# Scores of an attention block: two heads side by side in fp32r instead of one head in bf16 parts

## The reference

```python
q, k, v = (split_heads(einsum('bsd,kd->bsk', x, w)) for w in (wq, wk, wv))   # 16 heads of 8
scores = einsum('bhtc,bhkc->bhtk', q, k) * 8 ** -0.5
attn = softmax(where(causal, scores, -inf))
x = layernorm(x + einsum('bsv,dv->bsd', attn @ v, wo))
# mixture of experts: 64 experts of inner width 64, 8 chosen per token by grouped top-k, one shared expert
x = layernorm(x + sum_e coef_e * (silu(x @ Wg_e) * (x @ Wu_e)) @ Wd_e + shared(x))
```

## Time and profile before

| | |
|---|---|
| time, median of 3 runs | 1038.38 us (1034.61 to 1038.46) |
| the profiled execution | 1035.23 us, span of the core 1033.2 us |
| PE busy | 936.0 us (91%), 4800 matmuls |
| DVE busy | 810.7 us (78%) |
| POOL busy | 626.7 us (61%) |
| ACT busy | 462.3 us (45%) |
| mean granted clock of TensorE | 0.951 |
| DMA | 120.75 MB, 117 GB/s |

### The profile page before, as it was taken

One profiled execution on the slowest core, in us unless ns is written; L12 is line 12 of the kernel. 1 busy time (PEld: TensorE's weight loads), 2 busy tenths in 40 slices (PEclk: granted clock), 3 DMA queues, 4 the chain that ended last, 5 costly groups with the idle time before them and its releaser, 6 DMA issues.

```text
span 1033.2 us, 15722 instructions
## 1 busy us (share of the span) xinstructions
PE 936.0 (91%) x4800; PEld 564.4 (55%) x4800; DVE 810.7 (78%) x2435; ACT 462.3 (45%) x882; POOL 626.7 (61%) x668
## 2 busy tenths in 40 slices
PE   2687699999999899999999899999999999988996
PEld 1233356665566556665566556665566556655653
DVE  5765767798978997799977997798977986587554
ACT  2354345444444444445444444444444545433332
POOL 2432137665676556675676556675676667765775
PEclk7588689999999999999999999999999999999998
DMA  8441153332533253323533253322533232322331
GB/s 297 144 142 49 35 177 109 116 106 103 173 106 116 94 177 110 116 84 124 173 106 116 88 175 118 116 76 103 195 91 116 95 100 83 112 75 84 102 123 51
DMA packets 63075, 120.75 MB, mean 117 GB/s; under 512 B 7056, under 2 KB 34576, under 8 KB 62608
## 3 DMA queue, kind: packets, MB, share of 16 engines
q1 hardware_dynamic: 62992, 119.76, 36.0%
HBM read 97.32 MB, written 22.02 MB: 116 GB/s over the span
## 4 chain that ended last, share of the span: by engine, by line
PE 63%; DVE 27%; issue 4%; DMA 3%; POOL 2%; ACT 1%; SPq 0%; POOLq 0%; DVEq 0%
PE acc L594 8%; DVE max_out L890 7%; PE ob L541 7%; PE sm L511 5%; PE pu L472 5%; PE pg L472 5%; PE st L529 5%; PE pg L474 4%; PE pg L473 4%; PE pu L474 4%; PE pu L473 4%; DVE hid L963 4%; DVE hid L954 3%; PE acc L584 3%; PE acc L586 2%
## 5 line engine op out<-in xcount | busy, mean ns | idle before, releaser
L706 POOL TENSOR_TENSOR hid<-hid,coef_b 128x512 f32<-128x512 f32 x256 | 332.2, 1298 | 197.1 <-DVE hid L963 182.8
L655 ACT ACTIVATE hid<-pg 128x512 f32<-128x512 f32 x264 | 157.7, 597 | 359.9 <-PE pg L474 358.6
L890 DVE CUSTOM_DVE_ANT_0 max_out<-sm,causal_sb 128x128 bf16<-128x128 f32 (+3 forms) x512 | 235.6, 482 | 90.7 <-PE sm L511 89.3
L954 DVE SCALAR_TENSOR_TENSOR hid<-hid,pg 128x512 f32<-128x512 f32 x264 | 180.2, 682 | 86.9 <-ACT hid L655 86.9
L710 POOL TENSOR_TENSOR hid_lo<-hid,hid_hi 128x512 fp32r<-128x512 f32 x128 | 164.2, 1283 | 71.3 <-ACT hid_hi L662 70.0
L627 ACT ACTIVATE probs<-st 128x512 f32<-128x512 f32 (+1 forms) x384 | 187.1, 526 | 20.4 <-PE st L529 18.5
L963 DVE TENSOR_TENSOR hid<-hid,pu 128x512 f32<-128x512 f32 x256 | 174.6, 682 | 10.9 <-PE pu L474 6.2
L511 PE MATMUL sm<-k_stack,q_stack 72*128 72x128 bf16 (+3 forms) x512 | 140.9, 323 | 32.3 <-DMA k_stack<-k_rows_dram 16.5
L692 POOL TENSOR_SCALAR_AFFINE_SELECT probs<-probs 128x256 f32<-128x256 f32 x256 | 102.8, 426 | 75.4 <-ACT probs L627 74.9
L472 PE MATMUL pg<-x_hi,wg_hi 128*128 128x512 f32 x256 | 139.6, 545 | 9.8 <-DVE hid L954 9.7
L472 PE MATMUL pu<-x_hi,wu_hi 128*128 128x512 f32 x256 | 125.0, 488 | 15.7 <-DVE hid L963 15.6
(11 more groups left out here) (129 smaller groups left out, 1213.1 us busy)
## 6 DMA issues: line engine op xcount, KB each, us to landing
coef_b<-coef_dram SPq DMA_DIRECT2D x128, 512.0 KB, 3.9
q_rows_dram<-qk_parts SPq DMA_DIRECT2D x24, 384.0 KB, 3.3
k_rows_dram<-qk_parts SPq DMA_DIRECT2D x24, 384.0 KB, 3.7
q_stack<-q_rows_dram SPq DMA_DIRECT2D x64, 144.0 KB
k_stack<-k_rows_dram SPq DMA_DIRECT2D x64, 144.0 KB
xT_sb<-in_xT SPq DMA_DIRECT2D x8, 256.0 KB, 3.9
y<-in_x SPq DMA_DIRECT2D x8, 256.0 KB, 4.4
out<-out_sb SPq DMA_DIRECT2D x8, 256.0 KB, 2.4
```

The source lines that it names most:

```text
L706: pool.tensor_tensor(hid[:, i % 3, :], hid[:, i % 3, :], coef_b[:, half % 2, j, :], ALU.mult)\
L890: last = dve.tensor_tensor_reduce(out=max_out[:, seg.nth(BANK_SM, task) % 2, col:col + wide], in0=sm_of(seg, task)[:, col:col + wide], in1 ...
L954: dve.scalar_tensor_tensor(hid[:, i % 3, :], hid[:, i % 3, :], 1.0, pg[:, :], ALU.add, ALU.mult).then_inc(a_done, 1)
```

## The change

- q and k are split into two fp32r parts, not three bf16 ones: four products, 32 rows of contraction. ACT writes the first part, DVE the second in one subtraction straight into the part; the second split task is gone (`qlo`, `klo` only store).
- The maxima become two parts of rows (34 rows for `st`), kept in fp32 up to the transpose, and written as fp32r. `mn` has two steps, not four.
- The stacks are fp32r, 128 partitions high: the even head of a pair lies at partition 0, the odd one at 64. SP loads a pair with four DMAs instead of two, a group's maxima with two instead of one.
- For each part of `mx` and `st`, PE runs both heads of the pair together, alternating between the two positions, each head into its own bank. Both banks of `sm` (or `st`) are filled by one part of a pair, and the next such part waits until both are free.
- The places pair the heads: part p of both heads stands where part p of a head at twice the pace would.

Core of the diff:

```diff
-CONSTS = 5
+CONSTS = 3
-PARTS = 3
+PARTS = 2
 QK_ROWS = PARTS * PARTS * C
-STACK = 96
+ROWS = QK_ROWS + PARTS
+TILE = 64
-GROUP = dict(mn=(-0.22, -0.15, 0.02, 0.14), mT=0.42, pv=0.05, ot=0.67, on=0.99)
-PACKED_GROUP = dict(mn=(-0.22, -0.2, -0.13, 0.19), mT=0.42, pv=0.1, ot=0.57, on=1.19)
+GROUP = dict(mn=(-0.22, 0.02), mT=0.42, pv=0.05, ot=0.67, on=0.99)
+PACKED_GROUP = dict(mn=(-0.2, 0.0), mT=0.42, pv=0.1, ot=0.57, on=1.19)
...
     for h in range(NH):
-        out += [(max_at + (h + off) * pace, "mx", 3 * h + part) for part, off in enumerate(head["mx"])]
-        out += [(st_at + (h + off) * pace, "st", 3 * h + part) for part, off in enumerate(head["st"])]
-        out.append((st_at + (h + head["mask"]) * pace, "mask", h))
+        first, second = h - h % 2, h % 2
+        out += [(max_at + (first + 2 * off) * pace + 1e-6 * (2 * part + second), "mx", 3 * h + part)
+                for part, off in enumerate(head["mx"])]
+        out += [(st_at + (first + 2 * off) * pace + 1e-6 * (2 * part + second), "st", 3 * h + part)
+                for part, off in enumerate(head["st"])]
+        out.append((st_at + (first + 2 * head["mask"] + 0.15 * second) * pace, "mask", h))
...
-        qk_parts = sb("qk_parts", [P, 2, PARTS, S], BF16)
-        rest = sb("rest", [P, S])
-        q_stack = sb("q_stack", [STACK, RING, S], BF16)
-        k_stack = sb("k_stack", [STACK, RING, S], BF16)
+        qk_parts = sb("qk_parts", [P, 2, PARTS, S], F32R)
+        q_stack = sb("q_stack", [P, RING_PAIRS, S], F32R)
+        k_stack = sb("k_stack", [P, RING_PAIRS, S], F32R)
...
-                        hs, j = slice(2 * i, 2 * i + 2), i % RING_PAIRS
-                        for stack, dram in ((q_stack, q_rows_dram), (k_stack, k_rows_dram)):
-                            sp.dma_start(stack[0:QK_ROWS, 2 * j:2 * j + 2, :],
-                                         dram[par, :, :, :, hs].rearrange("a b c h t -> (a b c) h t"))\
-                                .then_inc(stacked[j], 16)
+                        j = i % RING_PAIRS
+                        for half in range(2):
+                            for stack, dram in ((q_stack, q_rows_dram), (k_stack, k_rows_dram)):
+                                sp.dma_start(stack[TILE * half:TILE * half + QK_ROWS, j, :].bitcast(F32),
+                                             dram[par, :, :, :, 2 * i + half].rearrange("a b c t -> (a b c) t"))\
+                                    .then_inc(stacked[j], 16)
...
-                            mm = pe.matmul(sm[:, col:col + wide], q_stack[0:QK_ROWS, h % RING, qb * P:(qb + 1) * P],
-                                           k_stack[0:QK_ROWS, h % RING, 0:wide], start=True, stop=True)
+                        if h % 2 == 0:
+                            other = ("mx", n, i + 3)
+                            bank_free(pe, seg, sm_free, BANK_SM, other, banks=2)
+                            col, j = 0, h // 2 % RING_PAIRS
+                            for qb in MX_PARTS[part]:
+                                wide = (qb + 1) * P
+                                for half, psum in enumerate((sm, sm_of(seg, other))):
+                                    at = TILE * half
+                                    mm = pe.matmul(psum[:, col:col + wide],
+                                                   q_stack[at:at + QK_ROWS, j, qb * P:(qb + 1) * P],
+                                                   k_stack[at:at + QK_ROWS, j, 0:wide], start=True, stop=True)
...
+                        if h % 2 == 0:
+                            other = ("st", n, i + 3)
+                            bank_free(pe, seg, exp_done, ("st",), other, banks=2)
+                            col, j = 0, h // 2 % RING_PAIRS
+                            for kb in ST_PARTS[part]:
+                                wide = S - kb * P
+                                for half, psum in enumerate((st_of(seg, task), st_of(seg, other))):
+                                    at = TILE * half
+                                    mm = pe.matmul(psum[:, col:col + wide],
+                                                   k_stack[at:at + ROWS, j, kb * P:(kb + 1) * P],
+                                                   q_stack[at:at + ROWS, j, kb * P:S], start=True, stop=True)
...
-                        bank_free(dve, seg, parts_done, ("q", "k"), task)
-                        dve.tensor_tensor(rest[:, :], sm_of(seg, task)[:, :], qk_parts[:, kind == "k", 0, :],
+                        parts = qk_parts[:, kind == "k"]
+                        dve.tensor_tensor(parts[:, 1, :], sm_of(seg, task)[:, :], parts[:, 0, :].bitcast(F32),
                                           ALU.subtract).then_inc(sm_free, 1)
```

109 lines of the change are left out of this document (43 added, 66 removed).

## The result

The changed kernel takes 1136.5 us against 1038.4 us (medians), a ratio of 1.097 with a 95% interval of 1.093 to 1.101. That is slower, as forecast, but 52 us beyond the forecast of 1084 us and 6.5 us outside the range of 1010 to 1130 us. The profiled execution's span is 1134.3 us, 101 us more than before.

What follows compares the result with a forecast made beforehand. PE was taken as the bound after the prologue. 1035.2 us profiled + 100 shape changes - 52 streams - 10 waits + 8 prologue = 1081, with 3.1 to the median 1084 us; forecast band 1060 to 1100, range 1010 to 1130.

Steps and rivals of the forecast that it cites:

- After the prologue PE is the bound: Steady state: PE busy 114.5 of 120 us, DVE 103.8, so PE was taken as the bound.
- The sign that I gave, PE busy near 99% in steady state: Expected in the PE timeline after the change, with each batch some 6 us longer.
- Streams, 1.32 us a pair: PE's mx and st score products: 1.32 us a pair, 1.02 less than before; 52 us saved over 304 visits.
- halves side by side: PE's two row halves of a pair stream and load weights together, so a pair pays each width once.
- rival (c): PE's halves don't load or don't stream together: 24 to 64 us more, 1110 to 1150 us; chance 0.13.
- Changes of shape, 0.19 us each: PE after the prologue: 527 more tile-shape changes, each 0.09 plus 0.10 us, together 100 us.
- (a): Row shapes change freely on PE: 996 us, range 985 to 1010; chance 0.18.
- (b): PE drains at shape changes but the load is fetched during it: 1036 us, range 1025 to 1050; chance 0.14.
- So I take nothing, except ... 10: DVE's lighter work counted as nothing, except 10 of PE's 25.3 us waits for the MoE products go.
- PSUM: costs nothing in steady state: Score banks: MoE products between visits cover the wait for both banks; up to 30 us if cover falls.
- rival (d): Visits wait for both banks in steady state too: up to 30 us on top, 1095 to 1115 us; chance 0.10.
- The prologue, +8 with a bound of +18: Before MoE work, engines take turns on the banks, some 0.5 us a visit: +8 us, bounds -5 and +18.

Runs made afterwards that it cites:

- the control with short maxima: Kernel before, with each query tile's maximum taken over its last 128 keys only; 1016.9 us.
- single heads: Changed kernel's row tiles and fp32r parts, but heads one by one with the places and single-bank visits of the kernel before; 1190.2 us, ratio 1.149.
- own bank: Changed kernel, with the second head waiting for its PSUM bank only just before its first matmul, not both banks before the visit; 1136.4 us.
- the two full-height fp32r kernels: Two fp32r parts padded to full height: in paired visits (changed kernel without row halves) 1123.6 us; heads singly in the places of before 1042.3 us.
- b early: Changed kernel with b, DVE's product that frees pu, placed right behind its u; 1133.3 us.
- joined: Kernel with mx and st in one tile shape, plus each st pair moved next to the nearest mx pair after the prologue; 1139.1 us.
- one shape: Changed kernel with a row of zeros added to mx (33 rows), so mx and st share the 64-row tile; 1134.9 us.
- short exponentials: Changed kernel with each exponential after the first four heads reading only 128 columns; 1130.2 us.
- short maxima: Each query tile's maximum over its last 128 keys only: in the changed kernel 1098.8 us, in the kernel before 1016.9, with paired places alone in bf16 1053.1.
- fp32r alone: Kernel before with two fp32r parts at full height, heads singly in the old places with single-bank waits; 1042.3 us, ratio 1.007.
- the kernel with the new places alone: Kernel before with only the order changed to paired places; bf16, full height, each head its own visit and bank; 1101.0 us, ratio 1.063.

## Why the forecast fell short

Three steps of the prediction failed. The prologue was put at +8 us and cost 41. DVE was put at nothing, less 10 us of waits, where PE's idle time grew. And the order of the tasks had no term at all, though it alone costs 65 us in bf16. The streams and the changes of shape, on which the sum was built, came out nearly as forecast and gave the direction rightly.

**Bound before.** "After the prologue PE is the bound": mostly. The profile's chain also runs over DVE around the routing, and the control with short maxima shows that less work on DVE shortens the batch (116.9 to 113.9 us). The sign that I gave, PE busy near 99% in steady state, did not come: after the first tanh it is 93.9%, where it was 94.3%.

**Streams, 1.32 us a pair** and **halves side by side**: right, as far as the visits show it: six take 3.5 us a pair, streams and changes together, against 3.30. The halves start 3 ns apart; rival (c) is out.

**Changes of shape, 0.19 us each**: right, as 0.09 in and 0.10 for the load in the timeline, 0.19 for one that was removed; over the 887 added to single heads it is 0.17 of PE's busy time and 0.15 of the span. Rivals (a) and (b) are out. PE's own work grew from 111.5 to 119.7 us a batch, 8.2; the forecast's 48 us over 304 visits (48 a batch) is 7.6.

**"So I take nothing, except ... 10"**: failed. Of the 25.3 us that PE waited for the MoE products I let 10 go, since a slower PE leaves DVE more time. They came to 28.4 us (26.8 for pu, 1.6 for pg). DVE had less to do, 96.5 us a batch against 100.4, and yet b came later, because it stood behind two heads' maxima. The forecast priced DVE by its total work and not by what stands in front of b in its queue.

**"PSUM: costs nothing in steady state"**: the reason was sound and the conclusion was not. The banks of the scores do stay covered (own bank: no gain), and rival (d), with its waits for row_max and probs, did not come: between 200 and 1000 us PE has none. The pairing costs 5.8 us a batch all the same, by the order alone, and I had no term for the order: places moved, engines' queues regrouped. In the changed kernel its 5.8 and the 8.2 of PE's work overlap to 9.4 us a batch.

**The prologue, +8 with a bound of +18**: the largest miss, 41.4. The mechanism was named (engines take turns), the size was not: I allowed 0.5 us a visit, 1.5 a pair, and it is 2.7 a pair (7.7 less 5.04) in the turn shown, and 37 us over eleven turns. Some 10 us of the 41 come with the fp32r parts and not with the pairing (10.4 with heads singly, 11.8 in pairs): each turn waits for a product that takes longer than in bf16, and I had counted the streams there as a gain. I let the clock stand where it was; it fell further, which costs little in the runs of the two full-height fp32r kernels and was not separated in this one.

By the marks, then: forecast 8 + 38 = 46 us, measured 41 + 60 = 101. What lies after the first tanh can be split into PE's work and its idle time (columns as in the earlier trace rows, first before, then after the change):

```profile
138.40:1033.20 894.80, 843.41 (x4314) 526.10 (x4313) 724.59 (x2073) 408.71 (x785) 585.98 (x607) 0.99 0.36 114
179.80:1134.30 954.50, 896.04 (x4313) 529.30 (x4311) 701.26 (x1995) 412.75 (x785) 580.32 (x607) 0.99 0.32 104
```

PE is busy 52.6 us longer, against +48 forecast, and idle 7.1 us longer (51.4 to 58.5), against -10. Of the 55 us missing, 33 are in the prologue, 17 in PE's idle time and 5 in its work. This is an account of where the time lies, not of what removing it would give: b early took 7.1 us out of the waits of three batches and the time stayed.

The batch stays at 126.1 to 126.4 us when PE's work falls by 2.8 us (joined), when b is early, and when ACT's work is cut; DVE's maxima move it. For b early and one shape the runs show where it goes, into unit 25 with its wait for x and the clock; for the short exponentials, and for the rest of what the joined pairs save, the chain that sets the batch was not isolated. And 36 us of the places' cost, which short maxima leave, have no shown cause.

Of the kernels that take the full maxima none beats the one before. The nearest is fp32r alone, at a batch 1.0 us shorter (0.7 us where the clock does not fall) and a prologue 10 us longer. The control with short maxima is 1.9% faster than the kernel before (0.981, 0.979 to 0.983), by leaving out the maximum over the earlier keys.

## What to carry to other kernels

Price a regrouping as an edit of its own: write out, for each in-order engine, what now stands ahead of the one operation that frees the bank of the engine that bounds, not only how much work the engine has. When two units of work share a visit, their readers get their work in twos, and where nothing else lies between (a prologue) the engines take turns; measure one turn, in whole, before sizing it. Before packing a contraction of 32 rows into half of the array, count the changes of tile shape: here each pair saved 1.0 us of streams by the sum and paid for ten changes. And compare small savings only between stretches of the same granted clock, since one fall of it takes about as much as such an edit gives.

## What the runs showed of the hardware

After a wait the clock can charge again. Behind PE's 2.03 us of idleness at 517.9, in the kernel with the new places alone, six fp32r products of 512 columns take 2.67 us (519.92 to 522.59), not 6 by 0.235. Table by stretch, columns as in the earlier trace rows, just before the wait and just after it:

```profile
515.00:517.00 2.00, 2.00 (x12) 0.98 (x10) 2.00 (x4) 0.85 (x3) 1.00 (x1) 1.00 0.92 347
...
519.90:523.00 3.10, 3.08 (x8) 2.00 (x9) 2.39 (x6) 0.00 (x0) 2.24 (x3) 0.52 0.00 0
```

The granted clock is 1.00 (2.4 GHz) before and 0.52, near the lower level of 1.2 GHz, over the 3.1 us that follow. The six products lose 1.26 us (2.67 less 1.41) to the clock and the restart, beside the 2.03 us of the wait itself. That wait stands in six batches of this kernel, and the clock fell behind it in three. Behind a wait of 1.17 us, also in six batches, it fell in four with b early and in one with the changed kernel. So the wait alone does not tell it; what else does is open.

Going from a full-height fp32r product to the fp32 transpose of 32 columns (L529) showed no gap in the changed kernel (0.23 us from start to start), where going to the 48-column bf16 transpose of the kernel before cost 0.09. Why was not tried.
